# A decoder layer with sparse experts: the token routing rewritten, and idle products put ahead of TensorE's long waits

## The reference

```python
    logits = xt @ Wg.T
    topk_logits, topk_idx = jax.lax.top_k(logits, TOP_K)
    w = jax.nn.softmax(topk_logits, axis=-1)
    gates = jnp.zeros((T, N_EXPERTS), xt.dtype).at[rows, topk_idx].add(w)
    h = jnp.einsum('th,ehi->tei', xt, W1) + b1
    h = jax.nn.gelu(h, approximate=False)
    o = jnp.einsum('tei,eih->teh', h, W2) + b2
    y = jnp.einsum('te,teh->th', gates, o)
    return y.reshape(orig_shape)
x = _layernorm(x + _L0_attn_ref(x, ...), axis=-1)
x = _layernorm(x + _L0_xattn_ref(x, ctx_768, ...), axis=-1)
x = _layernorm(x + _L0_ffn_ref(x, ...), axis=-1)
```

## Time and profile before

| | us |
|---|---|
| median of 3 runs (693.26 to 694.91) | 694.81 |
| the profiled execution | 693.73 |
| its span, first to last instruction | 692.0 |
| PE busy in it | 603.4 |
| DVE busy | 530.1 |
| ACT busy | 407.9 |
| POOL busy | 303.2 |

### The profile page before, as it was taken

The page is one execution under the profiler, slowest core; times in us unless marked ns, Lnnn a source line. Parts: engine busy times, 40 slices in busy tenths (PEclk is TensorE's granted clock), DMA queues, the critical chain, the costliest instruction groups (busy, mean ns, idle before and its releaser), DMA issues. The chain is left out here.

```text
span 692.0 us, 13570 instructions
## 1 busy us (share of the span) xinstructions
PE 603.4 (87%) x5232; PEld 414.6 (60%) x5232; DVE 530.1 (77%) x930; ACT 407.9 (59%) x622; POOL 303.2 (44%) x363
## 2 busy tenths in 40 slices
PE   5989688887999799898987853899999999999984
PEld 2435344453444535454654543698989989988963
DVE  4687576528877688877757779699999999999725
ACT  3655578763466344455651313388888988987613
POOL 9311255545356244625452434325464642662223
PEclk9999999999999999999999995699999999999998
DMA  7407454394002900111020017578888779786264
GB/s 229 143 1 176 100 153 153 104 254 163 1 1 92 218 28 14 48 64 31 1 94 30 0 35 239 169 260 267 300 288 283 264 267 290 264 279 208 92 227 161
DMA packets 70992, 103.65 MB, mean 150 GB/s; under 512 B 4848, under 2 KB 56776, under 8 KB 69904
## 3 DMA queue, kind: packets, MB, share of 16 engines
q1 hardware_dynamic: 67184, 92.55, 42.3%
q0 software_dynamic: 3744, 10.23, 4.2%
HBM read 80.28 MB, written 22.41 MB: 148 GB/s over the span
## 5 line engine op out<-in xcount | busy, mean ns | idle before, releaser
L240 DVE TENSOR_REDUCE rowmax<-M 128x1 f32<-128x512 f32 (+3 forms) x176 | 104.6, 636 | 37.6 <-PE M L230 35.5
L681 ACT ACTIVATE probs<-R 128x1024 f32<-128x1024 f32 x80 | 80.4, 1028 | 51.2 <-PE R L1035 50.9
L213 PE MATMUL HB<-xT,w 128*128 128x256 f16 (+1 forms) x1104 | 107.8, 258 | 0.3 <-DVE xT L1615 0.3
L1770 PE MATMUL YB<-w,h 128*128 128x256 f16 x936 | 105.9, 273 | 0.1
L213 PEld LDWEIGHTS HB<-xT,w 128*128 128x128 f16 x1104 | 94.8, 98 | 11.2 <-DVE xT L1615 1.7
L1770 PEld LDWEIGHTS YB<-w,h 128*128 128x128 f16 x936 | 91.4, 98 | 10.8 <-issue 0.4
L543 POOL TENSOR_SCALAR_AFFINE_SELECT probs<-probs 128x256 f32<-128x256 f32 x128 | 49.6, 407 | 97.4 <-ACT probs L681 96.9
L1467 ACT ACTIVATE hf<-HB,b 128x256 f32<-128x256 f32 (+1 forms) x184 | 69.9, 445 | 37.0 <-PE HB L213 35.5
L1388 POOL DMA_INDIRECT scratch_ys<-y,dst x39 | 41.9, 1075 | 98.2 <-ACT y L1447 93.0
L1380 POOL DMA_INDIRECT xg<-scratch_xs,src x39 | 62.4, 1601 | 26.6 <-issue 10.9
L1642 DVE SCALAR_TENSOR_TENSOR h<-hf,h 128x512 f16<-128x512 f32 (+1 forms) x92 | 56.6, 616 | 3.2
(11 more groups left out here) (272 smaller groups left out, 1071.7 us busy)
## 6 DMA issues: line engine op xcount, KB each, us to landing
w1f<-in_W SPq DMA_DIRECT2D x23, 1024.0 KB, 7.6
w2f<-in_W SPq DMA_DIRECT2D x23, 1024.0 KB, 6.0
scratch_qk<-qk SPq DMA_DIRECT2D x18, 256.0 KB, 3.0
scratch_ax<-stage SPq DMA_DIRECT2D x16, 256.0 KB, 2.5
scratch_vw<-stage SPq DMA_DIRECT2D x16, 256.0 KB, 2.9
vw<-scratch_vw SPq DMA_DIRECT2D x4, 1024.0 KB, 7.4
a_x<-scratch_ax SPq DMA_DIRECT2D x4, 1024.0 KB, 9.5
parts<-scratch_ys SPq DMA_DIRECT2D x8, 512.0 KB, 8.6
```

What stands on the lines that cost most here:

```text
L213: last = nc.tensor.matmul(out, left(a, k), right(b, k), start=(k == 0 and m == 0), stop=(k == n - 1 and m == 2))
L240: return nc.vector.tensor_reduce(rowmax[:, t, par * PAIRS + p0:par * PAIRS + p0 + pairs], bank[:, 0:pairs * wide].rearrange("p (n w) -> p ...
L681: A.activation(probs[:, n % RING, :, :], bank[:, :, :], ACT.Exp, scale=1.0 / (QS * QS)).then_inc(empty, 1)
L1770: last = M.matmul(YB[q][:, t, :], h[:, q, a, m, t * 128:t * 128 + 128], w2[:, q, b, m, :], start=((m, a, b) == (0, 0, 0)), stop=((m, a) == ...
```

## The change

In the attention block: the router's seventh pair is taken into `ORDER` (`rt:6:0`, `lg:6:0`, with ten idle products behind the logits), and its best two experts are searched at the start of the next block (`TOPPED` = 6 pairs are searched in the first block, `EARLY` = 7 have their logits there). A dictionary `WARM` puts 13, 8, 8 and 5 idle products ahead of the steps `VW:0:0`, `m:2:0`, `m:3:0` and `s:0:18`.

In the expert block: one late pair instead of two; idle products on PE ahead of the router's products (3), behind them (9), ahead of `stacked` (6) and ahead of the map (9). The running sums over experts become one product with a triangle `sum_upto` and one reduction. VectorE's chain for `eid` and its chain for `pos` are interleaved, each step waiting only for what it reads (`mark`). `in_row` and `in_half` are formed from a grid of row numbers, all operands f16, laid out so that the eight pairs of a set are innermost; PE then reads them with a step of eight elements. The product with the token number moves from GpSimd to VectorE, the doubling of the first choice behind the first set. GpSimd writes the grid as integers (`iota`), ScalarE copies it to f16. `stacked` is cleared by ScalarE (identity times zero) and not by GpSimd. The idle products between those of the map go. The first biases go into another bank.

```diff
-EARLY = (NB - 1) * NQ // 2
+TOPPED = (NB - 1) * NQ // 2
+EARLY = TOPPED + 1
...
-xe:3:3 xs:3:3 n:3:2 O:3:2 tp:0:0 tp:1:0 idle:228:3 O.d:3:2 xp:3:3 T:3:6 T.l:3:6 T:3:7 T.l:3:7 O:3:3 tp:2:0 tp:3:0
-tp:4:0 tp:5:0 O.d:3:3 r:3:3 n:3:3
+xe:3:3 xs:3:3 n:3:2 O:3:2 tp:0:0 tp:1:0 idle:228:3 O.d:3:2 xp:3:3 T:3:6 T.l:3:6 T:3:7 T.l:3:7 rt:6:0 rt.l:6:0 O:3:3
+tp:2:0 tp:3:0 lg:6:0 idle:251:10 O.d:3:3 r:3:3 tp:4:0 tp:5:0 lg.l:6:0 n:3:3
 """
+
+
+WARM = {("VW", 0, 0): (13, ("even", 1, 0)), ("m", 2, 0): (8, ("even", 2, 0)), ("m", 3, 0): (8, ("even", 3, 0)),
+        ("s", 0, 18): (5, ("ct", 0, 2))}
...
+        def keep_running(many, use):
+
+            bank, _ = opened(g, *use)
+            for _ in range(many):
+                M.matmul(bank[:, :].rearrange("p (n w) -> p n w", w=128), ident16[:, :],
+                         ident16[:, :].unsqueeze(1).to_broadcast([128, 4, 128]), start=True, stop=True)
+
         pe.wait_ge(consts, 1)
         for kind, b, n in STEPS:
+            if (kind, b, n) in WARM:
+                keep_running(*WARM[kind, b, n])
...
-    b1B = HB[3][:, 1, 0:FM * TILES].rearrange("p (m n) -> p m n", n=TILES)
+    b1B = YB[1][:, 0, 0:FM * TILES].rearrange("p (m n) -> p m n", n=TILES)
...
-        P.memset(stacked[:, :, :], 0.0).then_inc(share_step, 1)
         P.memset(b2f[:, :], 0.0).then_inc(b2_zero, 1)
+        P.iota(grid_i[:, :, :], pattern=[[1, 128], [0, ROWS_AT_ONCE]], base=0, channel_multiplier=0).then_inc(grid_made, 1)
...
-        pool.wait_ge(halves_found, 1)
-        for c in range(2):
-            ct = slice(c * NT, c * NT + NT)
-            P.tensor_tensor(in_half[:, 0, ct, :], in_half[:, 1, ct, :],
-                            token_f[:, c, :].unsqueeze(2).to_broadcast([128, NT, BLOCKS]),
-                            ALU.mult).then_inc(halves_set, 1)
...
+        A.activation(stacked[:, :, :].rearrange("p t w -> p (t w)").rearrange("p (n w) -> p n w", w=128),
+                     ident16[:, :].unsqueeze(1).to_broadcast([128, NT * STACKED // 128, 128]), ACT.Copy, scale=0.0
+                     ).then_inc(stacked_zero, 1)
         act.wait_ge(gap_done, 1)
         A.activation(gate[:, 1, :], gap[:, :], ACT.Exp).then_inc(gexp_done, 1)
 
         act.wait_ge(consts, 7)
         A.activation(table[:, :], iota_e[:, 0:1], ACT.Gelu)
+        act.wait_ge(grid_made, 1)
+        A.activation(flat(grid[:, :, :]), flat(grid_i[:, :, :]), ACT.Copy).then_inc(grid_done, 1)
...
+        top_two(TOPPED * 2, EARLY * 2)
+        top_index(TOPPED * 2, EARLY * 2)
...
-        after(V.tensor_copy(upto[:, 0, :, :], tiles_e[:, :, :]))
-        at = 0
-        for k in (1, 2, 4):
-            V.tensor_copy(upto[:, 1 - at, :, 0:k], upto[:, at, :, 0:k])
-            after(V.tensor_tensor(upto[:, 1 - at, :, k:], upto[:, at, :, k:], upto[:, at, :, 0:NE - k], ALU.add))
-            at = 1 - at
...
+        after(V.tensor_tensor(counted[:, :, :, :], wide(tiles_e[:, :, :].unsqueeze(2), 2, NE, NE),
+                              wide(sum_upto[:, :, :].unsqueeze(1), 2, NE, NE), ALU.mult))
+        after(V.tensor_reduce(upto[:, :, :], counted[:, :, :, :], AX.X, ALU.add))
...
+        ahead_at = mark(V.tensor_tensor(ahead[:, :, :], upto[:, :, :], tiles_e[:, :, :], ALU.subtract))
+        below_at = mark(V.tensor_tensor(below[:, :, :, :], wide(upto[:, :, :].unsqueeze(2), 2, TILES + 1, NE),
+                                        wide(iota_t[:, :, :].unsqueeze(3), 2, TILES + 1, NE), ALU.is_le))
+        edge_at = mark(V.tensor_scalar(edge[:, :], tiles_e[:, 0, :], float(SLOTS), None, ALU.mult))
+        dve.wait_ge(rt_step, ahead_at)
+        jump_at = mark(V.scalar_tensor_tensor(jump[:, :], upto[:, 0, :], 2.0, ahead[:, 1, :], ALU.mult, ALU.add))
+        dve.wait_ge(rt_step, below_at)
+        eid_at = mark(V.tensor_reduce(eid_f[:, :, :], below[:, :, :, :], AX.X, ALU.add))
...
-        rows_f = row_f[:, :, :].rearrange("p c t -> p (c t)")
-        for k in range(2 * NT // ROWS_AT_ONCE):
-            at_k = slice(k * ROWS_AT_ONCE, (k + 1) * ROWS_AT_ONCE)
-            V.tensor_tensor(in_row[:, at_k, :], wide(iota_r[:, :].unsqueeze(1), ROWS_AT_ONCE, 128),
-                            wide(rows_f[:, at_k].unsqueeze(2), ROWS_AT_ONCE, 128), ALU.is_equal).then_inc(placed, 1)
+        after(V.tensor_tensor(in_half[:, 1, :, :, :], wide(grid[:, 0:BLOCKS, :].unsqueeze(1), ROW_SETS, BLOCKS, ROWS_AT_ONCE),
+                              sets(half_16[:, :], BLOCKS), ALU.is_equal))
+        V.tensor_tensor(in_half[:, 0, :, :, :], in_half[:, 1, :, :, :],
+                        sets(token_16[:, :, :].rearrange("p c t -> p (c t)"), BLOCKS), ALU.mult).then_inc(halves_set, 1)
+        for k in range(ROW_SETS):
+            rows = row_16[:, k * ROWS_AT_ONCE:(k + 1) * ROWS_AT_ONCE].unsqueeze(1)
+            V.tensor_tensor(in_row[:, k, :, :], grid[:, :, :], wide(rows, 128, ROWS_AT_ONCE), ALU.is_equal).then_inc(placed, 1)
+            if k == 0:
+                dve.wait_ge(halves_set, 1)
+                first_choice = in_half[:, 1, 0:ROW_SETS // 2, :, :].rearrange("p k b j -> p (k b j)")
+                V.tensor_scalar(first_choice, first_choice, 2.0, None, ALU.mult).then_inc(halves_set, 1)
...
+        keep_running(3, 4)
         router(LATE - 1)
+        keep_running(9, 4)
...
+        keep_running(6, 4)
         pe.wait_ge(share_done, 3)
...
+        pe.wait_ge(turn_done, NT // NQ)
+        keep_running(9, 4)
+        pe.wait_ge(halves_set, 2)
+        for k in range(ROW_SETS):
+            pe.wait_ge(placed, k + 1)
+            for j in range(ROWS_AT_ONCE):
+                last = M.matmul(slot_map, in_row[:, k, :, j], in_half[:, :, k, :, j], start=(k, j) == (0, 0),
+                                stop=(k, j) == (ROW_SETS - 1, ROWS_AT_ONCE - 1))
```

More of the change, by code:

```diff
@@ L58 @@
 ROWS_AT_ONCE = 8
+ROW_SETS = 2 * NT // ROWS_AT_ONCE
 STACKED = 72
@@ L1206, in expert_block, with early @@
     shift = sb("shift", [128, NT])
+    with ExitStack() as routing_only:
+        def early(name, shape, dt):
+            return routing_only.enter_context(nc.sbuf_tensor(name, shape, dt))
+        grid_i = early("grid_i", [128, 128, ROWS_AT_ONCE], I32)
+        grid = early("grid", [128, 128, ROWS_AT_ONCE], F16)
+        in_row = early("in_row", [128, ROW_SETS, 128, ROWS_AT_ONCE], F16)
+        in_half = early("in_half", [128, 2, ROW_SETS, BLOCKS, ROWS_AT_ONCE], F16)
     parts = sb("parts", [128, NT, 2, D])
@@ L1515, in wide, with top_two, top_index @@
             return ap.to_broadcast([128, *shape])
+        def top_two(first, upto_tile):
+            for t in range(first, upto_tile):
+                last = V.max(top[:, t, :], logits[:, t * NE:t * NE + NE])
+            after(last)
+        def top_index(first, upto_tile):
+            for t in range(first, upto_tile):
+                last = V.max_index(topi[:, t, :], top[:, t, :], logits[:, t * NE:t * NE + NE])
+            return last
+        top_two(TOPPED * 2, EARLY * 2)
+        top_index(TOPPED * 2, EARLY * 2)
         for n in range(LATE):
@@ L1565, in _ @@
-        V.tensor_scalar(own_e[:, :], eid_c[0:NE, :], token_f[0:NE, 1, 0:1], None, ALU.is_equal).then_inc(own_done, 1)
-        V.tensor_tensor(ahead[:, :, :], upto[:, at, :, :], tiles_e[:, :, :], ALU.subtract)
-        after(V.tensor_scalar(edge[:, :], tiles_e[:, 0, :], float(SLOTS), None, ALU.mult))
-        after(V.scalar_tensor_tensor(jump[:, :], upto[:, at, 0, :], 2.0, ahead[:, 1, :], ALU.mult, ALU.add))
-        V.tensor_scalar(jump[:, :], jump[:, :], -128.0, 128.0 * (BLOCKS - 1), ALU.mult, ALU.add)
@@ L1571, in _ @@
-        run = rank.rearrange("p (t e) -> p t e", e=NE)
-        dve.wait_ge(ranks, 2)
-        after(V.tensor_tensor(past[:, :, :], run, wide(edge[:, :].unsqueeze(1), NT, NE), ALU.is_ge))
-        after(V.tensor_tensor(past[:, :, :], past[:, :, :], wide(jump[:, :].unsqueeze(1), NT, NE), ALU.mult))
-        after(V.scalar_tensor_tensor(pos[:, :, :], wide(ahead[:, 0, :].unsqueeze(1), NT, NE), float(SLOTS),
-                                     run, ALU.mult, ALU.add))
+        after(V.tensor_tensor(counted[:, :, :, :], wide(tiles_e[:, :, :].unsqueeze(2), 2, NE, NE),
+                              wide(sum_upto[:, :, :].unsqueeze(1), 2, NE, NE), ALU.mult))
@@ new lines, in _ @@
+        dve.wait_ge(rt_step, eid_at)
+        eid_at = mark(V.tensor_tensor(eid_c[:, :], eid_p[:, 0, :], eid_p[:, 1, :], ALU.add))
+        pos_at = mark(V.scalar_tensor_tensor(pos[:, :, :], wide(ahead[:, 0, :].unsqueeze(1), NT, NE), float(SLOTS),
+                                             run, ALU.mult, ALU.add))
+        dve.wait_ge(rt_step, eid_at)
+        V.tensor_scalar(eid[:, :], eid_c[:, :], NE - 1.0, None, ALU.min).then_inc(eid_done, 1)
+        dve.wait_ge(rt_step, max(jump_at, past_at))
@@ L1588, in _ @@
[L1588 to L1593 removed]
+        after(V.tensor_copy(half_16[:, :], half_i[:, :, :].rearrange("p c t -> p (c t)")))
@@ new lines, in _, with sets @@
+        V.scalar_tensor_tensor(row_16[:, :], half_16[:, :], -128.0, slot_f[:, :, :].rearrange("p c t -> p (c t)"),
```

(17 more changed lines are left out.)

79 lines of the change are left out of this document (39 added, 40 removed).

## The result

The changed kernel takes 693.57 us in the median of 20 runs, the kernel before, run between them on the same chips, 698.32 in the median of its 20. The ratio is 0.9921, 95% interval 0.9893 to 0.9949: by it the change saves 5.5 us. The profiled execution after took 694.56 us (span 692.8), the one before 693.73 (692.0); these two can't be subtracted, as will be seen. The forecast's direction holds, the gain was 5.5 and not 7.1 us, and the time lies 2.7 us above the range.

What follows compares the result with a forecast made beforehand. It took the routing's path of waits, mostly VectorE, and half-clock stretches of TensorE as the bound. Attention 1.5 plus routing 5.6 gave 7.1 us off the 694.81 median: 687.7 us, forecast 686.8 to 688.6, range 685.5 to 690.9.

Steps and rivals of the forecast that it cites:

- The level: Base of the forecast time: the gain is applied to the runs' median of 694.81 us, giving 687.7.
- Part 1: Attention block: idle products keep TensorE's clock up; 1.2 us at `VW:0:0` plus 0.3 at `m:3:0`, 1.5 us in all.
- Part 2: Seventh router pair moved into the attention block: cost 0, at most 0.2 us; second block 1.05 us shorter.
- Part 3: Routing's running sums as one triangle product and one reduction: 0.64 instead of 1.5 us, gain 0.86.
- Part 4: Routing, interleaved VectorE chains from `below` to `in_half`: 4.5 instead of 5.57 us, gain 1.1.
- Part 5: One-hot tables in dense f16: 0.73 us per 1024 elements, PE products 0.065 each, map complete 8 us earlier.
- Rival (d): VectorE's one-hot operations run one element at a time, 1.21 us each: `src` 1.8 us late, 689.5; chance 0.06.
- rival (c): PE's eight-element-step reads make map products dearer, up to 0.24 us each: `src` 3.2 us late, 690.9; chance 0.09.
- Rival (b): Clock low in the routing, so its idle products are in the way: `src` 3.0 us late, 690.7; chance 0.12.
- Where the gain is cut: Before the experts: W1's cast limits the gain to `src` to 6.2 to 6.3 us; gathers among weights cost 0.7.
- Routing in all: Second block up to the experts: 6.3 us gained to `src` less 0.7 for the gathers, 5.6 us.

Runs made afterwards that it cites:

- after_third: The changed kernel once more, unchanged, as yardstick beside the later variants: 688.03 us from 6 runs, ratio 0.9879 to the kernel before.
- no_idle_routing: The changed kernel without its 27 idle products in the routing: 694.19 us, ratio 0.9952 to the kernel before.
- gather_first: The changed kernel with SyncE issuing the second W2 and the b2 copies only behind the first two gathers: 694.11 us, ratio 0.9933 to the kernel before.
- by_two: The changed kernel with both one-hot tables and their grid interleaved by two elements instead of eight: 689.12 us, ratio 0.991 to the kernel before.
- no_warm: The changed kernel without the idle products in the attention block: 694.88 us, ratio 0.9981 to the kernel before.

## Why the prediction was right and wrong

**The level.** This is the step that put the time outside the range: "The median of the runs is 694.81, 1.1 above it; I apply the gain to the median". It was the median of three runs. The kernel before, run beside the changed one, has 698.32, 3.5 us more, and the time lies 2.7 us above the range; the range shifted by 3.5 us would have held it. In 116 runs of the kernel before, on all the chips, the median is 698.7 and 24 lie at or below 694.91, the highest of my three. Three such runs drawn at random would come about once in a hundred times (an estimate, 24/116 to the third power); whether it was luck alone is open. The profile was a lucky one as well: granted clock 0.969, where the runs' mean is 0.959. With 7.1 us off 698.7 the forecast would have been 691.6, and the changed kernel's 38 runs have a median of 692.3, the first 20 of them 693.57. The range held the bounds of the change and no bound for the base, though one of the three shown runs already differed by 1.6 us from another.

**Part 1**, 1.5 us: right for `VW:0:0` (1.2 forecast, 1.4 to 1.5 measured), and by the runs too small in the mean, since I counted only the two falls that my one execution showed. The runs' mean clock rises by 0.007 to 0.012 and the time falls by 3.2, 3.6 and 8.3 us; the two falls of the earlier trace rows, 6.4 us at half clock of 692, make 0.005 of that, so the rest, and probably the rest of the time, are other falls, of which the mean execution of the kernel before holds more than the one that I read. `m:3:0` can't be read: in three traces with its idle products (`after_third`, `no_idle_routing`, `gather_first`) there is a fall at 239.8 to 243 nevertheless.

**Part 2**, cost 0 to 0.2: 0.3 to 0.4. The last stretch of the attention block takes 109.8 us without and 110.2 with the moved router pair where it holds no fall, and 111.5 against 111.8 where it holds one. The gain in the second block was 0.6 and not 1.05: GpSimd's iota, which I had hidden "up to 2 us", fits its gap on GpSimd (1.41 us, until 421.81), but VectorE's copy of `topi` beside it takes 0.65 us and ends at 421.84, with the iota; in `by_two`, where the iota is over before, it takes 0.18. The cost of moved GpSimd work was looked for on GpSimd only.

**Part 3**, 0.86: 0.44 (2.34 us from `fits` to `below` before, 1.90 after). The product of 128 elements takes 0.55 us beside GpSimd's `share` products, where I had 0.29. **Part 4**: 5.57 to 4.37 us, forecast 4.5.

**Part 5**: VectorE's side is right (0.68 for 0.73, 0.80 for 0.85). Rival (d) falls, and the Trainium skill's two results a cycle for two 16-bit sources ("Vector Engine (DVE) Microarchitecture Reference", section 5.1) is what the trace shows: 1024 elements in 0.68 us and 1248 in 0.80, 0.54 ns an element more, where `in_row` and `fits` before give 1.03. PE's side is where it failed, by the mark that the prediction had set ("if PE's map products are over 0.14 us apart"): rival (c), to which I gave 0.09, is what happened, with 0.15 us where I kept 0.065. The wait for W1 hid most of it, as reckoned: `src` at 19.5 instead of 18.5, of which the iota has some 0.47 and the map the rest. Rival (b) needed a low clock in the routing; it was full until 434.9. What its idle products would cost at half clock no run shows: `no_idle_routing`, at 0.50, has none.

**Where the gain is cut**: "I add 0.7, bounds 0 and 2.2": 1.9, within the bounds, but 1.2 us more than I took. The row for it was there, 4.9 us in the median; I took a third of its distance with no reason but that the first gather is small. Routing in all: 5.6 forecast, 3.1 to 3.2 at the first expert product, 2.8 to 3.8 at the end of the experts. (The queues vary: in the traces of `no_warm` and `no_idle_routing`, with the same transfers, the cast of the second W1 starts 1.5 and 1.7 us earlier, the distance from gather to transposes is 5.0 us and the first expert product stands at 28.3 and 28.2.) Together with part 1's 3 or more, less part 2's 0.4, this makes about the 5.5 to 6.4 us measured, 5.5 by the ratio of the first 20 runs and 6.4 between the medians of all: the sum was near, its terms were off in both directions. That it was near is luck as much as reckoning, and with part 1 open between 2 and 8 us this sum checks nothing.

## What to carry to other kernels

Ask of the base what you ask of the change: when three runs and one profile are given, their level has a spread of its own, and the range has to hold it. When a layout is turned so that one engine reads densely, price the other engine's read of the same table, the moving operand of a product above all. When a step on a path is shortened, look at what already stands in the DMA queues when it ends: here an `src` 2.1 us earlier brought the first expert product forward by 0.5 us, and only with the weights held back by all of it. And a gain that a trace shows at the end of a stretch is not yet a gain in the kernel's time: where executions scatter by 10 us and more, a dozen runs don't show 3.

## What the runs showed of the hardware

- PE reads a moving operand of 78 f16 columns in steps of 16 bytes in 0.15 us, the same at 1.2 and at 2.4 GHz; in steps of 4 bytes 32 such products take 2.31 us together with the waits for their tables. With the moving operand dense, a stationary operand of 128 columns in steps of 16 bytes makes a product 0.06 us at full clock, in steps of 4 bytes 0.04.
- The clock falls at places that differ from one execution of a kernel to the next, also where PE has been busy (10.0 of 10.5 us ahead of the fall at 25.5): 17 us at half clock in the attention block of one, none in another.
- A VectorE copy of 32 elements beside a GpSimd iota of 1024 ended only with the iota: 0.65 us instead of 0.18. The searches just ahead of it, beside the same iota, kept their 0.16 us.
